# Layer 0's last subtraction on another engine, gathers in other places, and one more split step with a ring of four, in a recommender kernel

## What is computed

```python
e = stack([tbl_f[ids[:, f]] for f in range(39)], axis=1)        # (2048, 39, 16)
x0 = xk = e
for idx, (W, b) in enumerate(((w0, b0), (w1, b1), (w2, b2))):
    z = relu(einsum('bhd,bkd,hks->bsd', x0, xk, W) + b[None, :, None])   # s = 128
    if idx != 2:
        xk = z[:, :64, :]
        direct.append(z[:, 64:, :])
    else:
        direct.append(z)
z = sum(concatenate(direct, axis=1), axis=-1)                    # (2048, 256)
h = concatenate([z, dense_ctx], axis=1)
h = relu(h @ W_top1 + b_top1)
h = relu(h @ W_top2 + b_top2)
return h @ W_top3
```

## Time and profile before

| | before |
|---|---|
| median of 3 runs | 2597.91 us |
| the profiled execution | 2598.07 us |
| its span, first to last instruction | 2596.2 us |
| PE busy | 2443.5 us (94%) |
| DVE busy | 2169.6 us (84%) |
| POOL busy | 1875.1 us (72%) |
| ACT busy | 1661.3 us (64%) |
| mean granted clock of TensorE | 0.984 |
| DMA | 136 GB/s over the span |

### The profile page before, as it was taken

One profiled execution on the slowest core, in us unless ns is written; L12 is line 12 of the kernel. 1 busy time (PEld: TensorE's weight loads), 2 busy tenths in 40 slices (PEclk: granted clock), 3 DMA queues, 4 the chain that ended last, 5 costly groups with the idle time before them and its releaser, 6 DMA issues.

```text
span 2596.2 us, 32413 instructions
## 1 busy us (share of the span) xinstructions
PE 2443.5 (94%) x8654; PEld 1591.3 (61%) x8654; DVE 2169.6 (84%) x1872; ACT 1661.3 (64%) x2120; POOL 1875.1 (72%) x1270
## 2 busy tenths in 40 slices
PE   0899999999999999999999999999999999999989
PEld 0466666666656666666666666666666666666655
DVE  1588889889878888988988898898888888888880
ACT  1566666666666666766666676666666666666653
POOL 6578778777867777777787777778777777765450
PEclk6899999999999999999999999999999999999999
DMA  2677667667757766766776676677667666756730
GB/s 71 139 149 155 126 138 166 134 131 151 154 110 152 154 130 132 166 137 132 148 158 129 132 164 140 127 150 155 131 131 166 141 131 145 160 129 129 159 80 0
DMA packets 214715, 352.58 MB, mean 136 GB/s; under 512 B 34382, under 2 KB 47566, under 8 KB 214588
## 3 DMA queue, kind: packets, MB, share of 16 engines
q1 hardware_dynamic: 194717, 347.07, 61.6%
q0 software_dynamic: 19968, 5.15, 2.2%
HBM read 346.97 MB, written 5.12 MB: 136 GB/s over the span
## 4 chain that ended last, share of the span: by engine, by line
POOL 30%; issue 27%; PE 16%; DVE 9%; DMA 7%; ACT 7%; SPq 3%; POOLq 0%; ACTq 0%; DVEq 0%; another core or an unknown queue 0%
POOL emb L374 13%; POOL Pl L380 13%; DMA xb<-x_dram 7%; ACT Ph L514 5%; PE ps L807 5%; PE ps L797 4%; DVE P L692 3%; DVE ps L692 3%; PE ps L817 3%; POOL dir L404 3%; SPq L311 3%; DVE Pl L697 3%; PE ps L926 1%; PE ps L918 1%; POOL emb L385 1%
## 5 line engine op out<-in xcount | busy, mean ns | idle before, releaser
L380 POOL TENSOR_TENSOR Pl<-P,Ph 128x1024 fp32r<-128x1024 f32 x448 | 1072.3, 2397 | 479.1 <-ACT Ph L514 469.4
L692 DVE TENSOR_TENSOR P<-xb,ps 128x1024 f32<-128x1024 f32 x768 | 926.8, 1214 | 81.1 <-DMA xb<-x_dram 72.9
L807 PE MATMUL ps<-Ph,wh 128*128 128x512 f32 x1920 | 870.1, 459 | 8.1 <-ACT Ph L514 8.0
L697 DVE TENSOR_TENSOR Pl<-ps,Ph 128x1024 fp32r<-128x1024 f32 x512 | 626.1, 1223 | 178.9 <-ACT Ph L514 168.7
L374 POOL DMA_INDIRECT emb<-tbl_in,idx x624 | 601.0, 963 | 166.3 <-issue 145.3
L807 PE MATMUL ps<-Ph,wl 128*128 128x512 f32 x1792 | 707.4, 395 | 0.0
L514 ACT ACTIVATE Ph<-ps 128x1024 fp32r<-128x1024 f32 x512 | 523.3, 1022 | 285.3 <-DVE ps L692 217.3
L817 PE MATMUL ps<-Pl,wh 128*128 128x512 f32 x1920 | 689.7, 445 | 11.4 <-POOL Pl L380 11.3
L514 ACT ACTIVATE Ph<-P 128x1024 fp32r<-128x1024 f32 x448 | 474.6, 1059 | 325.3 <-DVE P L692 303.8
L692 DVE TENSOR_TENSOR ps<-xb,ps 128x1024 f32<-128x1024 f32 x512 | 628.2, 1227 | 28.1 <-DMA xb<-x_dram 10.2
L797 PE MATMUL ps<-P,wp 128*128 128x512 f32 x1280 | 603.7, 594 | 4.1 <-DVE P L692 4.1
(11 more groups left out here) (64 smaller groups left out, 826.7 us busy)
## 6 DMA issues: line engine op xcount, KB each, us to landing
xb<-x_dram SPq DMA_DIRECT2D x1280, 256.0 KB, 8.5
emb<-tbl_in,idx POOLq DMA_INDIRECT x624
x_dram<-rows_sb SPq DMA_DIRECT2D x64, 78.0 KB
xb<-w_in SPq DMA_DIRECT2D x15, 128.0 KB
xb<-wt_in SPq DMA_DIRECT2D x2, 512.0 KB, 8.6
xb<-dense_in SPq DMA_DIRECT2D x1, 768.0 KB, 5.9
wp<-w_in SPq DMA_DIRECT2D x5, 128.0 KB
xb<-w0a_in SPq DMA_DIRECT2D x1, 448.0 KB
```

Of the source, the lines that this page charges most:

```text
L380: pool.tensor_tensor(Pl[:, h_slot(ref, c, k)], P[:, p_slot(ref, c, k)], Ph[:, h_slot(ref, c, k)], ALU.subtract).then_inc(low_pool, 1)
L692: dve.tensor_tensor(p, xb[:, x], xk.unsqueeze(1).broadcast_to([128, 2, N]), ALU.mult)\
L697: dve.tensor_tensor(Pl[:, h_slot(ref, c, k)], p_ps, Ph[:, h_slot(ref, c, k)], ALU.subtract)\
L807: pe.matmul(z_of(c, k), w[:, q, j, :], Ph[:, h_slot(ref, c, k), j, :], start=k in (L1B, L2) and i + j == 0, stop=False)
```

## The change

1. `KIND[10]` goes from P to V: layer 2's first step is split, with its product in PSUM.
2. `HRING` goes from 5 to 4. The dense features get a buffer of their own (`dense0`) instead of a slot of the ring.
3. The subtraction of layer 0's rest moves from DVE to POOL. ACT writes the exact square to SBUF (in rows of the tensor that also holds `rows_sb`) and the PSUM bank is free after that. POOL subtracts at step 16 (`REST_AT`), behind low(15).
4. The gathers follow a table: 9, 10, 11 and 9 of them in chunks 0 to 3. `next_ids` moves from the start of chunk 2 to step 18 of chunk 1, and the first two gathers of the next set stand there, ahead of low(19). `full_emb` moves from step 15 to 17.
5. At the start, `low_emb(0)` runs on DVE, PE issues 36 matmuls that nobody reads (`WARM`) ahead of its first wait for embeddings, and the sums of chunk 0 go to three PSUM banks, rest first. In chunk 1 the rest comes first too. 13 gathers of tile 1 come early instead of 12.

```diff
-KIND = "GVPVGPVGVPPGVGVGVPVG"
+KIND = "GVPVGPVGVPVGVGVGVPVG"
-PRING, HRING = 4, 5
+PRING, HRING = 4, 4
-REST_AT = 1
+REST_AT = 16
-HIGH_AT, FULL_AT, LOW_AT = 15, 15, 17
+HIGH_AT, FULL_AT, LOW_AT = 15, 17, 17
-GATHER_AT = [k for k in range(STEPS) if KIND[k] != "G"]
+NEXT_IDS_AT = (1, 18)
+GATHERS = [[1, 2, 3, 5, 9, 14, 16, 17, 18], [1, 2, 3, 5, 6, 8, 9, 10, 18, 18],
+           [1, 2, 3, 5, 6, 9, 10, 12, 14, 16, 17], [1, 2, 3, 5, 6, 8, 9, 10, 17]]
...
+        early_ps = (ps[:, 6, :], ps[:, 7, :], aux_ps, ps[:, 7, :], aux_ps, ps[:, 7, :], aux_ps)
...
+            def rest_low(T, chunk):
+                pool.wait_ge(rest_high, T * CPT + chunk + 1)
+                pool.wait_ge(rest_square, T * CPT + chunk + 1)
+                pool.tensor_tensor(sqx[LOWS, :], rest_sq, sqx[LOWS, :], ALU.subtract).then_inc(rest_ready, 1)
...
-            low_emb(0)
...
-            early = 12
+            early = 13
...
+                        if k == REST_AT and not (last and c >= 2):
+                            rest_low(T, c + 2)
+                        if (c, k) == NEXT_IDS_AT and todo[2]:
+                            next_ids(T + 2)
+                        part = min(c, 1) if (c, k) < NEXT_IDS_AT else 2
+                        n = GATHERS[c].count(k) * (1 + (first and c == 0))
+                        for f in todo[part][:n]:
+                            gather(f)
...
+            def rest_squares(T, chunk, number, bank=aux_ps):
+                act.wait_ge(aux_ready, T * PER["aux"] + number + 1)
+                act.activation(sqx[:, :], bank[0:REST0], ACT.Square).then_inc(rest_high, 1)
+                act.activation(rest_sq, bank[LOWS], ACT.Square).then_inc(rest_square, 1)
...
-            rest_low(0, 0)
+            dve.wait_ge(emb_high, 1)
+            dve.tensor_tensor(emb2[:, :, 1, :], emb[:, :, :].rearrange("p f d -> p d f"),
+                              emb_h[:, :, :].rearrange("p f d -> p d f"), ALU.subtract).then_inc(emb_low, 1)
+            rest_low(0)
...
-                        if k == REST_AT and not end and not (first and c == 0):
-                            rest_low(T, c + 1)
...
+            for i in range(WARM):
+                pe.matmul(z1_ps[:, 0], wp[:, 0, 0, :], wp[:, 0:2].rearrange("p q j m -> p (q j m)"), start=True, stop=True)
...
-                            pe.wait_ge(aux_read, aux + 2 + t)
-                            contract0(t, c % 2)
+                            if t < FULL0:
+                                pe.wait_ge(aux_read, aux + 2 + t)
+                            else:
+                                pe.wait_ge(rest_ready, T * CPT + c + 3)
+                            contract0(t, c % 2, opens, t == T0 - 1)
```

More of the change, by code:

```diff
@@ L431, in tile @@
             def tile(T, ref, fields, first=False, last=False):
+                todo = [list(f) for f in fields]
                 for c in range(CPT):
[L434 to L437, removed]
                     for k in range(STEPS):
@@ L440, in tile @@
                             low(T, ref, c, k)
[L441 to L445, removed]
+                        if k == REST_AT and not (last and c >= 2):
[6 more added lines that the diff above has]
+                            gather(f)
+                        todo[part] = todo[part][n:]
                         if c == 0 and not first and k in FOLD1_AT:
@@ L463, in tile @@
                             low_emb(T + 1)
-            cuts = (0, 12, 21, 30, NF)
-            third, fourth, first, second = (range(a, b) for a, b in zip(cuts, cuts[1:]))
-            tile(0, 0, (range(early, 30), range(30, NF), third, fourth), first=True)
+            late, soon = len(GATHERS[0]), len([k for k in GATHERS[1] if (1, k) < NEXT_IDS_AT])
+            cut = NF - late - soon
+            assert sum(map(len, GATHERS)) == NF
+            start, middle, rest = range(0, cut), range(cut, cut + late), range(cut + late, NF)
+            tile(0, 0, (range(early, cut + late), rest, start), first=True)
             with pool.Fori(1, TILES - 2) as T:
-                tile(T, 1, (first, second, third, fourth))
-            tile(TILES - 2, TILES - 2, (first, second, (), ()))
-            tile(TILES - 1, TILES - 1, ((), (), (), ()), last=True)
+                tile(T, 1, (middle, rest, start))
+            tile(TILES - 2, TILES - 2, (middle, rest, ()))
+            tile(TILES - 1, TILES - 1, ((), (), ()), last=True)
             pool.wait_ge(z2_read, chunks)
@@ L537, in _ @@
                 copy_x(0, AUX * g)
-                for t in range(T0):
-                    square(0, AUX * g + 1 + t, t)
-                    s = t - (T0 - PRE - 1)
+                if g:
+                    rest_squares(0, 1, AUX + 1)
+                for t in range(FULL0):
+                    square(0, AUX * g + 2 + t, t, aux_ps if g else early_ps[t + 1])
+                    if t == 0 and not g:
+                        rest_squares(0, 0, 1, early_ps[0])
+                    s = t - (FULL0 - PRE)
                     if g and 0 <= s < PRE and KIND[L1B + s] != "P":
```

108 lines of the change are left out of this document (64 added, 44 removed).

## The result

The changed kernel takes **2661.05 us** (median of 4 runs, 2657.03 to 2662.11), the one before 2597.3 beside it (4 runs, 2593.55 to 2600.87): ratio 1.0246, 95% interval 1.0234 to 1.0259, so it is slower by 64 us. The forecast of 2624 had the sign and the place right, but the size too small: the time lies 9 us above the range's end of 2652.

The account below looks back on a forecast made before the run. PE was taken to bound the kernel, 94% busy, with the DMA train 0.90 us behind. Terms +14 +17 −6 +5 −5 +1 = +26 on 2598.07 gave 2624 us, range 2546 to 2652.

Parts of the forecast that it names:

- The queue on POOL in chunk 1: POOL's subtraction, `low_emb`, index copy and two gathers delay low(19); PE stands 4.1 us, period 2.7 longer; tiles sum to +14 us.
- A: Rival: POOL is on time, so the stall in chunk 1 vanishes: 2549 us, chance 0.15.
- D: Rival: POOL is late by half, some 2 us of stall in chunk 1, no clock fall: 2578 us, chance 0.12.
- The clock: PE's idle in chunk 1 can halve its clock once a tile, costing 1.2 us on average: +17 us.
- C: Rival: POOL is late in chunk 1 but PE's clock stays up: 2607 us, chance 0.20.
- E: Rival: PE's clock falls at every stall, by the full price of 3.5 us: 2656 us, chance 0.08.
- What an ordinary chunk gains: PE's lost 0.81 us goes, then step 4's input by DMA is late next: 0.7 us gained a chunk.
- DVE's wait for `xb` grows: Sign that the forecast is right: DVE waits longer for its transferred inputs; no size given.
- Step 10, P to V: Splitting step 10 saves PE 0.35 us a chunk; DVE gets 1.22 more, on no path by itself.
- The start: Warming gains nothing, `low_emb(0)` on DVE saves 1.2, three PSUM banks 5: together −6 us.
- Tile 0's chunk 0: Six gathers between low(15) and low(19) make low(19) 6 us late: +5 us with the tile's own gain gone.
- the ring of four: A rounding must find the low part of four split steps earlier done; 3.7 us to spare: 0, up to 0.5 a chunk.

Follow-up runs that it names:

- run 2: The changed kernel with four extra float32 matmuls on PE in chunk 1, where it waits for POOL: 2632.3 us, ratio 1.0136.
- run 1: The changed kernel with the index copy and its first two gathers moved back into chunk 2, behind low(19) and low(0): 2585.39 us, ratio 0.9954.
- run 6: run 1's kernel with the subtraction of layer 0's rest back on DVE, behind step 1's product: 2691.29 us, ratio 1.0367.
- run 3: run 1's kernel with the first four transfers of each train at half their columns from the third chunk on (output not the reference's): 2551.63 us.
- run 11: run 9's kernel with the first four transfers of each train at half their columns from the third chunk on (output not the reference's): 2516.03 us.
- run 8: run 1's kernel with `low_emb` two steps earlier and chunk 0's gathers of steps 16 to 18 moved ahead: 2572.86 us, ratio 0.9909.
- run 9: run 8 and run 5 together, so POOL's queue cleared and step 10 unsplit: 2557.5 us, ratio 0.986.
- Run 12: run 9's kernel with as many gathers as possible moved between steps 5 and 9, where no train of transfers runs: 2567.27 us, ratio 0.9885.
- run 5: run 1's kernel with step 10 unsplit again (V back to P): 2567.07 us, ratio 0.9893.
- run 10: run 9's kernel without the 36 warming matmuls (`WARM = 0`): 2559.99 us, ratio 0.9867.

## Why the prediction was right in sign and wrong in size

**The queue on POOL in chunk 1: right.** Forecast: subtraction 1.3, low(19) of chunk 1 ends at +24.9, chunk 0's at +21.9, PE wanting it at +20.8. Measured: 1.281, PE's low(19) at +25.14 and +21.74, and +20.63 in chunks 2 and 3 (medians of 12 chunks each). Without the clock the period of chunk 1 costs 3.0 more than before (run 2); 2.7 was forecast. Runs 1 and 2 exclude A and D: POOL was neither on time nor late by half.

**The clock: a step that failed.** "A fall costs between 0 and 3.5; I take 1.2 on average." It measured 1.84 a tile by run 2's traces, and 2.05 by its times (28.75 / 14), and the fall came in 13 of 14 tiles. In the chunk shown above, from low(19) to the next step 10 it takes 1298.08 − 1279.68 = 18.4 us; in the same chunk of run 2, 15.8, and the forecast had 15.5. I had discounted the fall because 4 us of idle "is little beside" the stretch in the earlier trace rows. That was a misreading: PE's idle in that stretch is a single stall of 4.83 us, hardly longer than the 4.1 that I forecast. The trace of the kernel before shows it (PE's timeline, just inside the window of 763 to 770 us):

```profile
765.84 1.22 PE L817 MATMUL ps<-Pl,wh 128*128 128x512 f32 x2 [4.83 <-POOL Pl L380]
```

The forecast so rested on a wrong length for the one fall in the loop that it had to go by. The fall falsifies C, and speaks for E's mechanism, at less than its price of 3.5. On whether the clock falls, E's sentence from the Trainium skill (TensorE: Matmul & The Clock Gate, Part 1) was near the truth here: all 13 stalls of 4.2 to 4.5 us brought the fall. Not every stall brings a fall, however: the one of 3.47 us didn't, about half of the 2.0 us ones of run 6 didn't, and none of 1.0 us in run 1 did. E's total of 2656 lies 5 us from the measured 2661, and that is chance: its clock was too dear by 1.66 a tile, 23 us in all, and the other terms, the ordinary chunks (16) above all, were too cheap by about as much. Together with the 3.0, chunks 1 cost 13 us more than I had summed: 4 of them POOL's lateness (3.0 for 2.7), 9 the clock (1.84 for 1.2).

**What an ordinary chunk gains: wrong in chunk 2, half wrong in chunk 3.** This is the other step that failed, and in us the larger one. The mechanism stands: PE's lost time went and the train bound next (runs 3 and 11). The size was "I take 0.7", and chunks 2, 3 and those without gathers together gave 9 where 25 were forecast: 16 us. Two things are behind it. First I took the 0.90 between PE and step 4's input from one chunk. Over the trace of before, the median in chunks 2 is 0.68, with step 4's product at +25.47, not +24.9. Second, I held the train's end fixed, and it moved. In the changed kernel step 4's product is at +25.85 there, 0.38 later. From it to the next step 10 it takes 11.92 in place of 12.30, 0.38 less: what PE gained behind step 4 the train took back ahead of it. My sign for this, that DVE's wait for `xb` grows, did not come: 83.1 us before, 77.5 after (products to `P` and to PSUM together). The one that did is PE's, whose first high matmul of step 4 now follows its rounding by 0.05 in chunks 2 and 3, where it came 0.68 and 0.84 later. A chunk 2 of it, DVE's, ACT's and PE's timelines in turn (step 10's product at 1141.38, the next at 1179.37; answers to the earlier trace rows):

```profile
1167.45 1.22 DVE L714 TENSOR_TENSOR P<-xb,ps 128x1024 f32<-128x1024 f32 x1 [1.25 <-DMA xb<-x_dram]
```

```profile
1168.78 1.06 ACT L530 ACTIVATE Ph<-P 128x1024 fp32r<-128x1024 f32 x1 [0.78 <-DVE P L714]
```

```profile
1169.89 0.50 PE L834 MATMUL ps<-Ph,wh 128*128 128x512 f32 x1 [1.33 <-ACT Ph L530]
```

DVE waits 1.25 for the transfer, ACT 0.78 for DVE and PE 1.33 for ACT: the whole chain hangs on the DMA, and PE's 1.33 is more than the 0.81 that the change had taken away. Why the train ends later isn't settled. Removing the split moves it by −0.17 in chunks 2 (run 8 to run 9) but by +0.33 in chunks 1. Run 12 points to gathers, in chunk 0 alone; but the number of gathers in those 24 us of chunks 2 is lower after (7) than before (8), so it doesn't explain this shift.

**Step 10, P to V: wrong.** It was put at 0.35 of PE gained and "on no path by itself" for DVE. In runs 5 and 9 its removal gains 18 and 15 us. PE's gain is given to POOL in chunks 0 and 1 and to the train in 2 and 3, and DVE's part costs 0.12 a chunk at the next step 10 (run 5). The prediction had the stretch from step 4 to step 10 as PE's low(4) and ACT's hand-over alone; DVE's subtraction of step 8 stands behind them as its last link.

**The start: wrong by 4.6.** −6 was forecast, 5 of it from the three banks; it gave −1.4. Warming gave nothing that could be told (run 10). In the window of 54 to 62 us ahead of the first transposes the clock has fallen again (0.66, after 1.00 in 20 to 54), so those four still take 1.04, where they took 1.05. The banks' part was not tried alone. By the two traces PE's second transposes come 3.8 us earlier (74.98 for 78.74), but the third only 1.6 (98.70 for 100.32), so most of what the start of chunk 0 gave was gone again one chunk later. Tile 0's chunk 0, the last chunks, the end and the ring of four were within 2 us each.

Sum of the misses: 13 (chunk 1) + 16 (chunks 2, 3, without gathers) + 4.6 + 1.4 (start, first chunk) − 2 (chunk 0) = 33, which is 59 − 26.

## What to carry to other kernels

When work is moved to an engine with free time, read that engine's queue at the moment its next result is wanted, not its share of busy time: POOL was 72% busy, and a copy and two gathers ahead of one subtraction, in one chunk of four, cost 75 us. Price an added stall of PE as the stall plus a clock fall, unless rows of the same kernel show stalls of that length without one, and read the length of such a stall from PE's timeline, not from the width of a window. And before a gain is booked on "the next bound stands x behind", take x as a median over chunks, and ask whether the change itself delays that bound.

## What the runs showed that I had not expected

- PE's stalls of 2.0 us (run 6) bring the granted clock to half in about every second chunk, those of 4.2 to 4.5 us (after) each time, the one of 3.47 us (after, tile 1) not, those of 1.0 us (run 1) not.
- The move of one DVE operation of 1.22 us, far ahead in the chunk, decides what the rest's subtraction costs on DVE: 0.9 of stall a chunk without the split (the kernel before), 2.0 with it (run 6), and then half clock on top.
- Some gathers, 113 or a multiple of it apart, start 2 to 7 us late with nothing in the profile to wait for. In the kernel before these are the 227th, 340th, 453rd and 566th; POOL's timeline at the first of these:

```profile
758.71 0.95 POOL L374 DMA_INDIRECT emb<-tbl_in,idx  x1 [7.12 <-issue]
759.96 0.96 POOL L374 DMA_INDIRECT emb<-tbl_in,idx  x1 [0.30 <-issue]
```

The changed kernel has them at its 114th, 227th, 453rd and 566th (3.2, 4.4, 5.3 and 3.0 us). Most of the single chunks of 39 to 44 us in the loop of traces that otherwise have 37 to 38 lie there, and this is the stretch of the earlier trace rows at 763 us. The cause is open. It costs the versions differently, as the same late gather stands before other work of POOL in each (a reading of the order that no run tested): tile 4's chunk 0 takes 43.7 before, 40.5 in the changed kernel, 40.9 in run 1 and 37.4 in run 8, so comparisons of two traces by a few us have to be made chunk by chunk.
